# Key bias from small TensorE products, query groups spread over the first pairs, and the FFN residual added by TensorE, in a cross-attention and FFN kernel

## The reference

```python
x = x + xattn(layernorm(x), ctx, ctx)      # x: 32 x 56 x 128, ctx: 32 x 1500 x 128
x = x + ffn(layernorm(x))

def xattn(x1, x2, x3):                     # one head of 128
    q, k, v = x1 @ Wq.T + bq, x2 @ Wk.T + bk, x3 @ Wv.T + bv
    return softmax(q @ k.T) @ v

def ffn(x):                                # 16 heads of 64, 8 experts, top 2
    q, k = per-head products of x with Wq, Wk
    w, sel = top_k(x @ Ws, 2)              # value mixture per token and head
    v = one_hot(sel) . sigmoid(w) . (x @ Wv)
    attn = softmax(q * 64**-0.5 @ k.T) @ v
    mask_o = one_hot of the top 2 of x @ Wd
    return sum over heads and chosen experts of attn @ Wo
```

## Time and profile before

| | us |
|---|---|
| median of three runs (486.66 to 654.05) | 486.81 |
| the profiled execution, whole | 487.15 |
| its span, first to last instruction | 485.4 |

### The profile page before, as it was taken

How to read it: one execution, slowest core, us unless ns; L and a number is a source line. 1 busy time by engine, 2 the same in 40 slices (tenths; PEclk the granted TensorE clock), 3 DMA queues, 4 the chain that set the end, 5 groups by cost and what they waited for, 6 DMA issues and landing times.

```text
span 485.4 us, 25548 instructions
## 1 busy us (share of the span) xinstructions
PE 411.0 (85%) x10763; PEld 357.7 (74%) x10763; DVE 412.8 (85%) x798; ACT 334.2 (69%) x904; POOL 140.1 (29%) x146
## 2 busy tenths in 40 slices
PE   1657789999999997477899899998989998989865
PEld 1546678898898877366877788777878787878654
DVE  5974988989989872778999999999999999999832
ACT  5665667887887835356876687668767776877661
POOL 7655886888888843000000000000000000000000
PEclk9987998999999999589999999999999999999995
DMA  7952664564551000000000000000000000000000
GB/s 183 362 170 99 197 210 133 172 215 135 195 194 65 1 1 1 2 3 3 3 8 0 5 5 5 0 5 5 5 0 5 5 2 2 5 5 0 7 7 11
DMA packets 18156, 29.49 MB, mean 61 GB/s; under 512 B 3016, under 2 KB 14024, under 8 KB 18120
## 3 DMA queue, kind: packets, MB, share of 16 engines
q1 hardware_dynamic: 18120, 28.97, 18.6%
HBM read 28.05 MB, written 0.92 MB: 60 GB/s over the span
## 4 chain that ended last, share of the span: by engine, by line
DVE 46%; PE 30%; issue 12%; ACT 8%; DMA 1%; DVEq 1%; SPq 1%; POOL 0%; ACTq 0%; POOLq 0%
DVE ctxf_all L986 8%; DVE ctxf_all L960 6%; PE ps L1086 5%; DVE ah L1014 4%; DVE attnf L997 3%; ACT pf L525 3%; PE ps L1322 2%; PE ps L1133 2%; PE ps L1119 2%; PE ps L1134 2%; PE ps L1135 2%; PE ps L1101 2%; PE ps L1357 2%; DVE eq L912 1%; DVE oh L933 1%
## 5 line engine op out<-in xcount | busy, mean ns | idle before, releaser
L626 ACT ACTIVATE e_sb<-ps,smn 128x56 f32<-128x56 f32 x256 | 76.0, 369 | 1.6 <-DVE smn L1004 1.6
L626 ACT ACTIVATION_READ_ACCUMULATOR e_sb<-ps,smn 128x1 f32 x256 | 67.1, 269 | 0.0
L986 DVE TENSOR_TENSOR ctxf_all<-mixp,diag_h 128x3584 f16<-128x3584 f16 x32 | 63.2, 2017 | 0.0
L395 POOL TENSOR_TENSOR nat<-ctxf_all,nat 128x640 f16<-128x640 f32 x32 | 54.5, 1702 | 27.0 <-ACT nat L514 27.0
L1086 PE MATMUL ps<-ident,nat 128*128 128x128 f16 x768 | 56.9, 225 | 2.7 <-ACT nat L514 1.4
L401 POOL TENSOR_TENSOR p<-pf,p 128x672 f16<-128x672 f32 x32 | 54.1, 1692 | 15.1 <-ACT p L528 14.9
L514 ACT CAST nat<-ctxf_all 128x1536 f16<-128x1536 f32 x32 | 47.4, 1482 | 8.3 <-PE ps L1135 5.5
L1086 PEld LDWEIGHTS ps<-ident,nat 128*128 128x128 f16 x768 | 46.5, 100 | 6.1 <-issue 5.4
L754 DVE COPY ctxT<-ps 128x1024 f16<-128x1024 f16 x64 | 42.5, 682 | 2.3 <-PE ps L1086 2.2
L525 ACT ACTIVATE pf<-ps 128x672 f32<-128x672 f32 x32 | 23.7, 740 | 25.5 <-PE ps L1119 25.5
L1257 PE MATMUL ps<-xn,mT 128*128 128x112 f16 x256 | 40.9, 218 | 0.0
(11 more groups left out here) (171 smaller groups left out, 1239.5 us busy)
## 6 DMA issues: line engine op xcount, KB each, us to landing
ctxf_all<-in_ctx_dram SPq DMA_DIRECT2D x32, 704.0 KB
ctxf_all<-in_ctx_dram SPq DMA_DIRECT2D x32, 46.0 KB
x_all<-in_x_dram SPq DMA_DIRECT2D x4, 224.0 KB
out_dram<-y_all SPq DMA_DIRECT2D x32, 28.0 KB
ctxf_all<-in_ctx_dram SPq DMA_DIRECT2D x32, 18.0 KB
fwq_nat<-in_L_ffn_Wq_dram SPq DMA_DIRECT2D x1, 512.0 KB, 6.0
fwk_nat<-in_L_ffn_Wk_dram SPq DMA_DIRECT2D x1, 512.0 KB, 6.7
fwv_nat<-in_L_ffn_Wv_dram SPq DMA_DIRECT2D x1, 256.0 KB, 6.6
```

The costliest lines, as they stand in the source:

```text
L395: pool.tensor_tensor(nat[k][:, 1, 7 * C:], ctxf[k][:, 7 * C:], nat[k][:, 0, 7 * C:], ALU.subtract).then_inc(natlo2, 1)
L626: last = act.activation(e_sb[:, k, b, 0:S], ps[:, b, S * k:S * k + S], ACT.Exp, bias=smn[:, K16 * b + k:K16 * b + k + 1], scale=-1.0, accu ...
L986: last = dve.tensor_tensor(dv[:, part, :, :, :], mixp[:, part, :, :].unsqueeze(2).broadcast_to((P, 2 * NQ, HALF, H)), diag_h[:, :, :].unsq ...
```

## The change

- The key bias: two products of one column give 128 coefficients down the partitions and the constant in a [128, 2] tile. Behind each group's query product, PE makes eight products of one column each: the weights are 64 columns of `xn1T` (one sequence and what follows it), the moving column is the coefficients, the result goes to four columns behind the queries in the same bank. ACT adds the constant as it copies these to `cq` (`qk_evac`). `bias_products` on GpSimd and `key_bias` on DVE are gone. `xn1T` is eight columns longer and is cleared once by DVE.
- Groups 2 and 3 of x: the turn and the copy of group 2 stand in step 0, its product, its query halves and the turn and copy of group 3 in step 1, the rest of group 3 in step 2. They use bank 7, which the maxima's turn uses as well, so `max_turn` of these steps waits for the query halves and for `cq`. DVE scales group 2 in step 0 and group 3 in step 1.
- GpSimd's four bv adds stand two ahead of step 0, one in step 1 and one in step 2. bv is loaded ahead of the second ctx tile.
- The FFN: PE adds the residual with a fifth f32 product, of the identity with the tile of `x_all`, and ACT copies the sum to `y_all` between its `tanh` and the copy of the attention sums (L685). DVE's addition (L1019) is gone.

```diff
--- before.py
+++ after.py
@@ -91,11 +91,10 @@
...
         wvT = sb("wvT", [P, C])
-        xn1T = sb("xn1T", [P, B * S])
+        xn1T = sb("xn1T", [P, B * S + SLOT - S])
         qk_all = sb("qk_all", [P, 2, B * S], F16)
         bk_rep = sb("bk_rep", [P, C])
-        bkq = sb("bkq", [P, C + 1])
-        cq_x = sb("cq_x", [P, NP])
+        bkq = sb("bkq", [P, 2])
         cq = sb("cq", [P, NP])
@@ -131,7 +130,7 @@
...
         xn16 = sb("xn16", [P, 2, 2 * S], F16)
-        z = xn1T[:, :].rearrange("p (h n) -> p h n", h=H)
+        z = xn1T[:, 0:B * S].rearrange("p (h n) -> p h n", h=H)
         g_sb = sb("g_sb", [P, 32, E])
...
@@ -284,7 +281,7 @@
...
         GC = NP * C // NG
-        T_BANK, Q_BANK = (2, 6, 6, 6), (7, 6, 6, 6)
+        T_BANK, Q_BANK = (2, 6, 7, 7), (7, 6, 7, 7)
         TURNS = ((1, 2, 4), (3, 5, 6))
@@ -320,9 +317,8 @@
...
             load(0, 0)
-            load(1, 1)
             sp.dma_start(bv_all[:, :], bv.rearrange("(o d) -> o d", o=1).broadcast_to((P, C))).then_inc(d_bv, 16)
-            for k in range(2, RING):
+            for k in range(1, RING):
                 load(k, k)
...
@@ -445,25 +433,20 @@
...
                     queries(u + 2, (s + 2) % DEEP)
+                    if isinstance(u, int) and 0 < u < DEEP:
+                        add_bv(u + 1)
                     low_rows(2 * u + 4, slot(s, 2, 0))
...
-            bias_products(0)
             low_rows(0, 0)
             low_rows(1, 1)
+            add_bv(0)
             queries(1, 1)
             low_rows(2, 2)
-            step(0, 0)
-            bias_products(1)
-            add_bv(0)
-            bias_products(2)
-            step(1, 1)
-            bias_products(3)
             add_bv(1)
-            step(2, 2)
-            add_bv(2)
-            add_bv(3)
+            for u in range(DEEP):
+                step(u, u)
             with pool.Fori(1, NP // DEEP - 1) as i:
@@ -496,6 +479,7 @@
...
+                act.wait_ge(x_pad, 1)
                 act.wait_ge(xt_pe, g + 1)
@@ -504,6 +488,8 @@
...
                 act.wait_ge(qk_pe, g + 1)
+                act.wait_ge(bkq_out, 1)
+                act.activation(cq[:, 4 * g:4 * g + 4], ps[:, Q_BANK[g], GW:GW + 4], ACT.Identity, bias=bkq[:, 1:2]).then_inc(cq_d, 1)
                 act.activation(qk_all[:, 0, GW * g:GW * (g + 1)], ps[:, Q_BANK[g], 0:GW], ACT.Identity,
@@ -529,28 +515,25 @@
...
             def step(u, s, i):
-                start = isinstance(u, int) and u == 0
+                start = isinstance(u, int)
+                if start and u == 0:
+                    x_evac(1)
+                if start and 0 < u < DEEP:
+                    qk_evac(u + 1)
                 if has(u + 1):
                     t_evac(2 * u + 2, u + 1, 0)
-                if start:
-                    x_evac(1)
+                if start and u == 0:
+                    qk_evac(1)
                 if has(u + 2):
                     split_hi(2 * u + 4, slot(s, 2, 0), i + (s + 2) // DEEP)
-                if start:
-                    qk_evac(1)
                 if has(u):
                     exps(0, u)
-                if start:
-                    x_evac(2)
+                if start and u < DEEP - 1:
+                    x_evac(u + 2)
                 if has(u + 1):
                     t_evac(2 * u + 3, u + 1, 1)
-                if start:
-                    qk_evac(2)
                 if has(u):
                     exps(1, u)
-                if start:
-                    x_evac(3)
-                    qk_evac(3)
                 if has(u + 2):
...
@@ -678,6 +661,9 @@
...
                     half_turns(i + 1)
+                if old:
+                    after(act, f_o, i - 1)
+                    act.copy(y_all[:, bass.ds((i - 2) * C, C)], ps[:, 3, 0:C]).then_inc(f_y, 1)
                 if back:
@@ -691,21 +677,23 @@
...
             half_turns(0)
-            iteration(0, back=False)
-            iteration(1)
+            iteration(0, back=False, old=False)
+            iteration(1, old=False)
             with act.Fori(2, NP - 1) as i:
...
             iteration(NP, front=False, nxt=False)
+            iteration(NP + 1, front=False, back=False, nxt=False)
...
             dve.memset(x_all[:, 2 * GC:], 0.0).then_inc(x_zero, 1)
+            dve.memset(xn1T[:, :], 0.0).then_inc(x_pad, 1)
             dve.wait_ge(d_w, 16 * NW)
...
             dve.wait_ge(w_pe, 3)
-            dve.tensor_copy(bkq[:, :], ps[:, 5, 0:C + 1]).then_inc(bkq_out, 1)
+            dve.tensor_copy(bkq[:, :], ps[:, 5, 0:2]).then_inc(bkq_out, 1)
...
@@ -763,6 +745,7 @@
...
                 dve.tensor_reduce(m_q[:, :], ps[:, 7, 0:P], AX.X, ALU.max).then_inc(mred, 1)
+                dve.wait_ge(cq_d, pair // 4 + 1 if isinstance(pair, int) and pair < 4 else NG)
                 dve.wait_ge(mred, pair + 1)
@@ -807,28 +790,28 @@
...
             def step(u, s):
-                start = isinstance(u, int) and u == 0
+                start = isinstance(u, int) and u < DEEP
                 if has(u):
                     tile_max(2 * u, u, 0)
+                if start and u > 0:
+                    qk_low(u + 1)
                 if has(u - 2):
...
                     tile_max(2 * u + 1, u, 1)
-                if start:
-                    ln_scale(3)
-                    ln_apply(3)
+                if start and u < 2:
+                    ln_scale(u + 2)
+                    ln_apply(u + 2)
                 if has(u + 1):
...
                     shifts(u)
-                if start:
+                if start and u == 0:
                     qk_low(1)
...
                     t_evac(2 * u + 2, u + 1, 0, 2)
-                if start:
-                    qk_low(2)
                 if has(u - 2):
@@ -842,8 +825,6 @@
...
                     t_evac(2 * u + 3, u + 1, 1, 2)
-                if start:
-                    qk_low(3)
@@ -855,26 +836,19 @@
...
             t_evac(0, 0, 0, 0)
-            ln_scale(2)
-            ln_apply(2)
-            t_evac(0, 0, 0, 2)
+            ln_stats(3)
             qk_low(0)
...
             dve.tensor_copy(qk_cur[0][:, :, :], qk_all[:, :, 0:2 * S]).then_inc(qkc, 1)
+            t_evac(0, 0, 0, 2)
             split_lo(1, 1)
             t_evac(1, 0, 1, 0)
-            key_bias(0)
-            ln_stats(3)
             t_evac(1, 0, 1, 2)
...
             dve.wait_ge(c_zero, 5)
-            step(0, 0)
-            step(1, 1)
-            key_bias(1)
-            key_bias(2)
-            step(2, 2)
-            key_bias(3)
+            for u in range(DEEP):
+                step(u, u)
             dve.wait_ge(cq_d, NG)
...
@@ -1014,10 +988,6 @@
...
                     top_two(i + 1)
-                if old:
-                    after(dve, f_o, i - 1)
-                    dve.tensor_tensor(y_all[:, bass.ds((i - 2) * C, C)], ps[:, 3, 0:C], x_all[:, bass.ds((i - 2) * C, C)],
-                                      ALU.add).then_inc(f_y, 1)
                 if front:
...
@@ -1048,14 +1017,14 @@
...
             pe.wait_ge(c_bk, 1)
-            pe.matmul(ps[:, 5, 0:C], bk_rep[:, :], wq_nat[:, :], start=True, stop=True)
-            pe.matmul(ps[:, 5, C:C + 1], bk_rep[:, :], bq_col[:, :], start=True, stop=True).then_inc(w_pe, 1)
+            pe.matmul(ps[:, 5, 0:1], wq_nat[:, :], bk_col[:, :], start=True, stop=True)
+            pe.matmul(ps[:, 5, 1:2], bk_rep[:, :], bq_col[:, :], start=True, stop=True).then_inc(w_pe, 1)
...
                 if g >= 2:
-                    pe.wait_ge(qk_lo, g)
+                    pe.wait_ge(mred, g - 1)
                 for k in range(4):
@@ -1065,7 +1034,14 @@
...
                 pe.wait_ge(xt_act, g + 1)
-                pe.matmul(ps[:, Q_BANK[g], 0:GW], wqk[:, :], xn1T[:, GW * g:GW * (g + 1)], start=True, stop=True).then_inc(qk_pe, 1)
+                pe.matmul(ps[:, Q_BANK[g], 0:GW], wqk[:, :], xn1T[:, GW * g:GW * (g + 1)], start=True, stop=True)
+                pe.wait_ge(bkq_out, 1)
+                for k in range(4):
+                    for b in range(2):
+                        n = 8 * g + 2 * k + b
+                        last = pe.matmul(ps[SLOT * b:SLOT * b + SLOT, Q_BANK[g], GW + k:GW + k + 1], xn1T[:, S * n:S * n + SLOT],
+                                         bkq[:, 0:1], start=True, stop=True)
+                last.then_inc(qk_pe, 1)
@@ -1150,48 +1126,46 @@
...
             def step(u, s):
-                start = isinstance(u, int) and u == 0
+                start = isinstance(u, int) and u < DEEP
                 if has(u):
-                    if not start:
+                    if not (start and u == 0):
                         scores(2 * u, u, s, 0)
+                if start and u > 0:
+                    x_qk(u + 1)
                 if has(u + 1):
...
                     scores(2 * u + 1, u, s, 1)
-                if start:
+                if start and u == 0:
                     x_turn(1)
...
                 if has(u - 1):
-                    if isinstance(u, int) and u == 1:
```

(48 more changed lines are left out.)

## The result

| | before | after |
|---|---|---|
| median, us | 488.17 | 468.54 (467.14 to 469.56) |
| ratio, with its 95% interval | | 0.961 (0.956 to 0.966) |
| the profiled execution, whole / span | 487.15 / 485.4 | 469.56 / 467.7 |
| mean granted clock of PE | 0.955 | 0.973 |

One of the four runs of before, at 654.05, is left out of the ratio; without it the median of before is 486.81.

A forecast was written before the change was run, and what follows sets the result against it. DVE's work was taken to bound the prologue and FFN loop, a chain of round trips step 0. Terms -1.0 - 7.4 + 0 - 0.9 - 0.2 - 2.6 + 0.5 = -11.6 took 487.15 to 475.5 us; range 471.5 to 481.

The forecast's parts named there:

- prologue: Before pair 0's first maximum: DVE loses group 2's scaling and the bias sums; -1.0 us (bounds -2 and +1).
- step 0: First attention pair: groups 2 and 3 mostly leave it, with their round trips; -7.4 us (bounds -4.5 and -9).
- FFN loop: DVE's residual addition goes in 13 iterations, 0.20 us each; -2.6 us (bounds 0 and -3.6).
- tail: Last output group at the kernel's end: two more PE records on the path; +0.5 us (bounds 0 and +1).
- step 3: Fourth attention pair, which ran partly at the lower clock level before; -0.2 us (0 to -0.7).
- Step 1: Second attention pair: bias sums go, group 3's scaling and group 2's low half come; 0 us (bounds -1.5 and +2.5).
- the rival: Prologue: two of GpSimd's bv adds each cost DVE 1.3 us through the shared port; 478.1 us, chance 0.1.
- Small products: PE's one-column key bias products behind each group's query product: 16 records, 0.5 us a group.
- dear price of 3.4: Rival: the one-column key bias products take 3.4 us a group instead of 0.5; 483.5 us, chance 0.08.
- rival of no gain: FFN iterations gain nothing, as DVE waits for a late PE or ACT instead; 478.1 us, chance 0.1.
- ACT's copies: Rival: query copies heading ACT's steps 1 and 2 cost 2 us more each; 479.5 us, chance 0.2.
- the slower case: FFN loop: ACT's new copy waits for late output products, losing 1.0 us an iteration; 491.2 us, chance 0.03.

The follow-up runs named there:

- before_again: The kernel before, unchanged, run once more: 482.75 us (one run).
- before_p50: The kernel before with 50 idle f32 products (200 instructions) in PE's wait for the first layer norm: 482.20 us, ratio 0.991.
- attn_only: The kernel before with all of the change but the FFN edit: 471.29 us, ratio 0.966.
- after_p31: The kernel after with 31 idle products (124 instructions) at the start: 475.06 us, ratio 0.974.
- after_bv1col: The kernel after with GpSimd adding bv to one column in 128 only: 467.27 us, ratio 0.959.
- small_only: The kernel before with the key bias by small products, query groups 1 to 3 still in step 0 and one bank: 482.32 us, ratio 0.991.
- ffn_only: The kernel before with the FFN edit alone: 484.08 us, ratio 0.996.
- after_lowlate: The kernel after with DVE's low half of the queries in steps 1 and 2 behind the second maximum: 469.63 us, ratio 0.967.
- before_pad440: The kernel before with 220 more PE instructions that only wait on a long-arrived semaphore, ahead of the first turn: 501.33 us, ratio 1.027.
- after_bvearly: The kernel after with GpSimd's third bv add moved to step 0 and the fourth elsewhere in step 1: 468.63 us, ratio 0.962.

## Why the prediction was wrong

By its own terms, in us, from the profiled executions of before and after:

| term | predicted | measured |
|---|---|---|
| prologue, step 0, 1, 2, 3 | -1.0, -7.4, 0, -0.9, -0.2 | -0.6, -10.2, +1.4, -0.7, -0.6 |
| attention half | -9.5 | -9.6 (-10.8 to pair 4; 1.2 given back up to the first `dv`) |
| FFN loop | -2.6 | -2.4 |
| tail | +0.5 | -5.6 |
| sum | -11.6 | -17.7 |

The steps are those of one execution each. Against before_again, steps 0 to 3 of the kernel after differ by -9.3, +1.4, -0.7 and +0.8, so the gain of step 3 is not shown, and that of step 0 is 9 to 10. The attention half's -9.6 is -7.0 against before_again, whose first `dv` comes at 203.06; the medians of before_p50 and attn_only, neither with a late stop, differ by 10.9.

**The step that failed is the tail:** "The last output group stands alone on the path: eight records in 2.08 us; two more are +0.5 (bounds 0 and +1)." It took all of the 31 us but this group as fixed. 3.07 us of them were two stops of PE for its own instructions, the 64 products behind the second took 3.21 instead of 1.78 at the lower clock level, and the 2.08 itself was a row at that level (0.91 after; the ten records for which 2.6 was forecast took 1.40). Without stops the edit's own part is small: 25.2 in attn_only against 25.4 after, +0.2. With the stops put back, the kernel after takes 475.06, and the forecast was 475.5. That it comes so close is in part luck: the attention half's -9.5 against -9.6 is a sum of errors that cancel (step 0's gain was put too low, step 1's loss and the 1.2 given back later at nothing), before_again moves it by more than that, and the padding of after_p31 brought two stops elsewhere. The range (its lower end is 471.9, not 471.5, by the three pieces it names) missed because it held no bound for this, though the chain of waits of before showed "issue" inside straight runs of products.

**Step 0** was below its bound of -9: I left 1.0 of short gaps and 2.1 of the round trip for group 1 on the path, and of both 0.66 of idle time was left. That the clock would be full there (0.77 before, 0.82 in before_again) I hadn't counted either.

**Step 1**, at 13.77, was within its bounds but over the 13 us that the prediction had named as a sign of being wrong, with ACT's query copy at its head. Both reasons given are in the rows (ACT's query copy behind the ctx conversion, GpSimd's bv add beside the scaling), but only for the second is a cost shown: 1.6 in the stage, by after_bv1col, where the add is all but left out. The rule of the Trainium skill (SBUF — State Buffer, Who interferes with whom) that was weighed there agrees with these rows: 2.88 from 39.87, beside GpSimd's add (39.40 to 40.68) and subtraction (40.76 to 42.16), and 1.12 without the add. It is not worth 2.6 in the total, as the rival had it.

**Small products:** sixteen records took 0.63 us behind the product of group 2 and 1.02 behind that of group 0, against 0.5 counted; the products stand 58 ns apart in groups 1 to 3 and 107 in group 0, where the prediction's sign of being wrong was 60. The dear price of 3.4 is out. But "DVE loses the four sums" was worth nothing by itself (small_only): what the sums gave back, step 0 and, in step 3, the bv adds took.

**FFN:** 16.29 an iteration, DVE busy 15.77; the covers on PE and ACT held, and the rival of no gain is out. ffn_only is at 0.996, with the stops still in its tail.

The other rivals: ACT's copies did come to stand ahead of DVE's low half (2.55 and 2.35 us), but after_lowlate shows that PE's scores end no earlier; the slower case didn't come near.

## What to carry to other kernels

Read the chain of waits through to the end of the kernel, and look for "issue" inside a straight run of equal instructions: that time, and the clock that falls behind it, belongs to no line of the kernel, and any edit that adds or drops instructions on that engine, however far ahead, can remove it or bring it in. Give it a bound on both sides, repeat the unchanged kernel to see how far its stages move by themselves, and when an edit's gain turns up at a place that it doesn't touch, pad the instruction stream by a known number before believing in the edit. A round trip that blocks an in-order queue can be worth more than an engine's busy time: here spreading it, with the bv adds moved, gave some 11 us by subtraction, and small products in place of 5.75 us of DVE's sums gave none.

## What was not expected of the hardware

- PE stopped for 2.06 to 2.24 us, some 2.4 us from the start of an instruction packet of 16 KB (16,384 bytes), at places that moved by 36 = 256 - 220 records with 220 more instructions, by 17 with the FFN edit, and by 100 with 100, and that lie 512 records apart where a kernel has two. The Trainium skill (Runtime: NRT & Kernel Launch, Instruction fetch mechanics) has the stream come in 16 KiB blocks of 256 instructions, which agrees, and calls the cost of a block's edge "mostly hidden"; here two edges and the clock behind them were some 5.5 us of 487 (a tail of 31.03 in the kernel before, of 25.5 in before_p50).
- A wait on a semaphore that had long arrived cost PE some 106 ns: in before_pad440 the trace has 219 of them, from 5.73 to 29.50 us, 106 ns apart in the median.
- DVE's four scalings of group 3 took 2.88 us in the kernel after and 3.40 in after_lowlate beside GpSimd's add and subtraction, 1.12 in after_bv1col and 1.11 in after_bvearly with the add cut down or moved.
